# Reordering the score matmuls of a second attention stage, and splitting every other exponential in two

## The reference

```
qkv = xf @ W_qkv + b_qkv
q, k, v = split(qkv.reshape(B, N, 8, 96))
attn = softmax(einsum('bihd,bjhd->bijh', q, k) * 32 ** -0.5, axis=2)
res = einsum('bijh,bjhd->bihd', attn, v).reshape(B, N, 256) @ W_out + b_out + xf
```

## Time and profile before

| | us |
|---|---|
| median of 3 runs | 1339.67 |
| lowest and highest of the runs | 1337.60, 1340.34 |
| the profiled execution | 1338.09 |
| its span, first to last instruction | 1336.3 |
| TensorE, VectorE, ScalarE, GpSimd busy | 1258.8, 779.1, 813.4, 685.3 |

### The profile page before, as it was taken

The page is one execution under the profiler, slowest core; times in us unless marked ns, Lnnn a source line. Parts: engine busy times, 40 slices in busy tenths (PEclk is TensorE's granted clock), DMA queues, the critical chain, the costliest instruction groups (busy, mean ns, idle before and its releaser), DMA issues.

```text
span 1336.3 us, 24965 instructions
## 1 busy us (share of the span) xinstructions
PE 1258.8 (94%) x10420; PEld 495.7 (37%) x10420; DVE 779.1 (58%) x1002; ACT 813.4 (61%) x912; POOL 685.3 (51%) x387
## 2 busy tenths in 40 slices
PE   6499999999999999999999998879999899999987
PEld 4332222222222222222222224634444655555543
DVE  6766666666666666666666665620002677777753
ACT  4677777787777778777777874442212355555552
POOL 3466666666666666666666663320000066656562
PEclk9599999999999999999999999989999999999999
DMA  2340111011011101101100100000006222222211
GB/s 73 96 135 1 33 32 25 9 33 33 1 33 33 24 10 33 32 2 33 33 24 10 33 1 1 0 0 0 0 1 229 93 53 56 57 57 57 67 27 71
DMA packets 22504, 51.63 MB, mean 39 GB/s; under 512 B 5622, under 2 KB 10870, under 8 KB 22264
## 3 DMA queue, kind: packets, MB, share of 16 engines
q1 hardware_dynamic: 20084, 43.74, 11.8%
q10 hardware_dynamic: 2308, 6.30, 1.9%
HBM read 36.64 MB, written 11.15 MB: 36 GB/s over the span
## 4 chain that ended last, share of the span: by engine, by line
PE 86%; ACT 6%; DVE 5%; issue 1%; DMA 1%; ACTq 0%; POOL 0%; POOLq 0%; SPq 0%; DVEq 0%
PE ps L936 33%; PE ps L945 18%; PE ps L1131 6%; PE ps L927 5%; ACT big L619 5%; PE ps L1142 5%; PE ps L1043 4%; PE ps L1053 4%; PE ps L1152 2%; PE ps L1072 2%; PE ps L1082 1%; PE ps L1030 1%; PE ps L1195 1%; DVE big L669 1%; PE ps L996 1%
## 5 line engine op out<-in xcount | busy, mean ns | idle before, releaser
L936 PE MATMUL ps<-big,w 64*64 64x512 f32 x4096 | 483.5, 589 | 0.0
L534 ACT ACTIVATE big<-ps 128x1024 f32<-128x1024 f32 x256 | 261.9, 1023 | 178.5 <-PE ps L936 178.5
L728 DVE TENSOR_SCALAR big<-big 128x1024 f32<-128x1024 f32 x256 | 177.7, 694 | 263.9 <-POOL big L435 263.9
L435 POOL TENSOR_TENSOR big<-qpad 128x1024 f32<-128x1024 f32 x128 | 244.6, 1911 | 146.5 <-PE ps L936 70.4
L722 DVE TENSOR_TENSOR big<-qpad,ps 128x1024 f32<-128x1024 f32 x256 | 310.9, 1215 | 7.3 <-ACT ps L513 5.4
L435 POOL TENSOR_TENSOR big<-qpad,V 128x1024 f32<-128x1024 f32 x128 | 244.4, 1910 | 129.4 <-PE ps L936 72.3
L534 ACT ACTIVATE big<-ps,vec 128x1024 f32<-128x1024 f32 x256 | 283.7, 1108 | 0.0
L945 PE MATMUL ps<-big,w3s 128*32 128x512 f32 x2048 | 246.2, 598 | 1.3 <-ACT big L534 1.3
L936 PEld LDWEIGHTS ps<-big,w 64*64 64x64 f32 x4096 | 146.5, 133 | 206.5 <-issue 112.4
L460 POOL TENSOR_TENSOR big<-big 128x1024 f32<-128x1024 f32 x32 | 76.2, 2382 | 238.6 <-ACT big L619 189.4
L619 ACT ACTIVATE big<-ps 128x1024 f32<-128x1024 f32 x128 | 130.9, 1024 | 107.4 <-PE ps L1131 90.9
(11 more groups left out here) (154 smaller groups left out, 977.7 us busy)
## 6 DMA issues: line engine op xcount, KB each, us to landing
raw<-s_f SPq DMA_DIRECT2D x32, 512.0 KB, 5.9
h1l<-k_d SPq DMA_DIRECT2D x33, 128.0 KB, 3.5
h1h<-q_d ACTq DMA_DIRECT2D x33, 128.0 KB, 4.1
X<-in_x SPq DMA_DIRECT2D x2, 1024.0 KB, 6.2
q_d<-XN SPq DMA_DIRECT2D x4, 512.0 KB, 3.2
k_d<-XN SPq DMA_DIRECT2D x4, 512.0 KB, 3.7
q_d<-big SPq DMA_DIRECT2D x4, 512.0 KB, 3.9
k_d<-big SPq DMA_DIRECT2D x4, 512.0 KB, 5.0
```

The source lines that it names most:

```text
L435: pool.tensor_tensor(h1[m % HRING].rearrange("p (y a b) -> p y a b", y=2, b=W), u.unsqueeze(2).to_broadcast(shape), a[:, :, HALF // W * hf ...
L534: act.activation(h2[m % H2RING], z2[m % ZRING], ACT.Relu, bias=v("cb2") if m % 2 else 0.0).then_inc(h2_ready, 1)
L728: dve.tensor_scalar(h1[m % HRING], h1[m % HRING], 0.0, None, ALU.max).then_inc(h1_ready, 1)
L936: last = pe.matmul(z2[m % ZRING][CH * y:CH * (y + 1), HALF * x:HALF * (x + 1)], w2[CH * x:CH * (x + 1), :], h1[m % HRING][CH * x:CH * (x + ...
```

## The change

The order of a round becomes across(2r), along(2r+14), across(2r+1), along(2r+15). The three pairs of banks still rotate by one with every product, so that the pairs are dealt out anew: along(2r+15) now takes the pair of across(2r), across(2r+1) that of the round before's along(2r+13), and along(2r+14) that of the round before's across(2r-1). In the rounds without along the two across slots take different pairs. The exponential of every even slot becomes two, of 128 x 512 each; the first signals a new semaphore `half_ready`, the second `pr_ready`. The two matmuls of an odd along wait for one of them each. The waits of across, along and turn are rewritten for the new pairs.

```diff
@@ -196,7 +196,7 @@
         vv_ready, vv_saved = sem("vv_ready"), sem("vv_saved")
         rT_in = [sem(f"rT_in{i}") for i in range(2)]
         st_in = [sem(f"st_in{i}") for i in range(HEADS3)]
-        added, sums_done = sem("added"), sem("sums_done")
+        added, sums_done, half_ready = sem("added"), sem("sums_done"), sem("half_ready")
         tr_ready, m_hi, m_lo, m_in, ones_ready, bo_ready, bo_saved = (
             sem(x) for x in ("tr_ready", "m_hi", "m_lo", "m_in", "ones_ready", "bo_ready", "bo_saved"))
         sc_ready, mx_ready, st_ready, pr_ready, pv_done, o_done = (
@@ -236,7 +236,7 @@
             if x < AHEAD_MAX:
                 return (x + turned(x)) % 2
             s = x - AHEAD_MAX
-            return (4 * (s // 2) + s % 2 + turned(x - x % 2)) % 3
+            return (4 * (s // 2) + 2 * (s % 2) + turned(x)) % 3
 
         def turn_pair(n):
 
@@ -245,7 +245,7 @@
 
         def across_pair(s):
 
-            return (4 * (s // 2) + 3 * (s % 2) + turned(s - s % 2 + AHEAD_MAX) - 1) % 3
+            return (4 * (s // 2) + 2 * (s % 2) + turned(s + AHEAD_MAX) - 1) % 3
 
         def plane_rows(t, first, n, a):
 
@@ -616,7 +616,11 @@
                 if s >= PRING:
                     act.wait_ge(pv_done, s - PRING + 1)
                     act.wait_ge(added, (s - PRING) // 2 + 1)
-                act.activation(PT[s % PRING], bank(2 * across_pair(s), 2), ACT.Exp).then_inc(pr_ready, 1)
+                if s % 2 == 0:
+                    act.activation(PT[s % PRING][:, 0:HALF], bank(2 * across_pair(s)), ACT.Exp).then_inc(half_ready, 1)
+                    act.activation(PT[s % PRING][:, HALF:N], bank(2 * across_pair(s) + 1), ACT.Exp).then_inc(pr_ready, 1)
+                else:
+                    act.activation(PT[s % PRING], bank(2 * across_pair(s), 2), ACT.Exp).then_inc(pr_ready, 1)
                 if s % NK == NK - 1 and HEADS3 <= s // NK + 3 < G:
                     load_queries(s // NK + 3)
 
@@ -1095,14 +1099,14 @@
                 elif x < 2:
                     pass
                 elif turning(x):
+                    pe.wait_ge(mx_ready, x)
+                elif x == AHEAD_MAX:
+                    pe.wait_ge(mx_ready, x - 1)
+                elif x % 2 == 0:
                     pe.wait_ge(pr_ready, x - AHEAD_MAX)
-                elif turning(x - 1):
-                    pe.wait_ge(m_lo, turned(x))
-                elif x % 2 == 0:
-                    pe.wait_ge(mx_ready, x - (x == AHEAD_MAX))
-                elif x > AHEAD_MAX + 1:
-                    pe.wait_ge(pr_ready, x - AHEAD_MAX - 1)
                 for hf in range(2):
+                    if x > AHEAD_MAX and x % 2 == 1:
+                        pe.wait_ge((half_ready, pr_ready)[hf], ((x - AHEAD_MAX + 1) // 2, x - AHEAD_MAX)[hf])
                     last = pe.matmul(bank(2 * along_pair(x) + hf), QS[n % HEADS3][0:ROWS, P * it:P * (it + 1)],
                                      KS[n % HEADS3][0:ROWS, HALF * hf:HALF * (hf + 1)], start=True, stop=True)
                 last.then_inc(sc_ready, 1)
@@ -1110,7 +1114,10 @@
             def turn(n):
 
                 pe.wait_ge(mx_ready, NK * (n + 1))
-                pe.wait_ge(mx_ready, min(TURN + NK * n - 1, SLOTS))
+                if n < G - 1:
+                    pe.wait_ge(mx_ready, TURN + NK * n - 1)
+                else:
+                    pe.wait_ge(pr_ready, TURN + NK * n - AHEAD_MAX - 2)
                 pe.transpose(bank(2 * turn_pair(n))[0:NK, 0:P], amax[n % HEADS3][:, :], ident[:, :]).then_inc(tr_ready, 1)
 
             def across(s):
@@ -1119,14 +1126,16 @@
                 if kt == 0:
                     pe.wait_ge(m_in, 32 * (n + 1))
                 x = s + AHEAD_MAX
-                if s % 2 == 1:
+                if turning(x):
                     pe.wait_ge(pr_ready, s)
-                elif x <= SLOTS:
-                    pe.wait_ge(mx_ready, x if turning(x) or s == 0 else x - 1)
-                else:
+                elif turning(x - 1):
+                    pe.wait_ge(m_lo, turned(x))
+                elif s == 0:
+                    pe.wait_ge(mx_ready, AHEAD_MAX)
+                elif s > 1 and x - 1 <= SLOTS:
+                    pe.wait_ge(mx_ready, x - 1)
+                elif s > 1:
                     pe.wait_ge(pr_ready, s - 2)
-                    if x == TURN + NK * (G - 1) + 4:
-                        pe.wait_ge(m_lo, G)
                 for hf in range(2):
                     last = pe.matmul(bank(2 * across_pair(s) + hf), KS[n % HEADS3][0:ROWS + 2, P * kt:P * (kt + 1)],
                                      QS[n % HEADS3][0:ROWS + 2, HALF * hf:HALF * (hf + 1)], start=True, stop=True)
@@ -1166,16 +1175,14 @@
             pe.wait_ge(vv_saved, 2 * NK)
             pe.wait_ge(ones_ready, 1 + HEADS3)
             for r in range(SLOTS // 2 + 2):
-                s, x = 2 * r, 2 * r + AHEAD_MAX
-                if turning(x):
-                    turn(turned(x) - 1)
-                if s < SLOTS:
-                    across(s)
-                if x < SLOTS:
-                    along(x)
-                    along(x + 1)
-                if s < SLOTS:
-                    across(s + 1)
+                for s in (2 * r, 2 * r + 1):
+                    x = s + AHEAD_MAX
+                    if turning(x):
+                        turn(turned(x) - 1)
+                    if s < SLOTS:
+                        across(s)
+                    if x < SLOTS:
+                        along(x)
                 if 0 < r <= SLOTS // 2:
                     weigh(2 * r - 2)
                     weigh(2 * r - 1)
```

## The result

The changed kernel takes 1319.9 us (median of four runs, 1316.65 to 1320.53) against 1338.95 for the kernel before in the same comparison (median of four, 1337.6 to 1340.34). The ratio is 0.9853, 95% interval 0.9833 to 0.9872: 19.05 us faster. The forecast was 18.8 us and 1320.9. The profiled execution of the changed kernel took 1319.84 us, its span is 1317.2.

A forecast was written before the change was run, and what follows sets the result against it. Taken as the bound: the exponential of across(2r), for which across(2r+1) waits. Gains of 8.8 + 0.8 + 9.2 = 18.8 us against the median of 1339.67 gave 1320.9 us, range 1314 to 1328.

The forecast's parts named there:

- What bounds the kernel: Second attention: across(2r+1) waits for the exponential of across(2r), which sets the 3.94 us round; along products cost nothing.
- Order and banks in rounds 2 to 56: Rounds with along: by the new order alone nothing is won; the wait moves from across(2r+1) to along(2r+15).
- The two halves: Rounds 2 to 56: only the second along matmul waits, weigh starts at 2.34 not 2.50; 0.16 us a round, 8.8 us.
- The two terms on which it rests: Even exponentials: a half takes some 0.60 us, and halves start 0.49 us apart.
- Halves without overlap: Rival, even exponentials: each half pays its whole 0.60, 0.05 us won a round, 1326.9 us; chance 0.11.
- Halves as cheap as the whole: Rival, even exponentials: two halves cost as much as the whole, 0.23 us won a round, 1317.0 us; chance 0.09.
- the slower case: Rival, even exponentials: TensorE writing the neighbouring bank slows the halves, weigh 0.30 us later than today, 1346.2 us; chance 0.04.
- its estimate of 1.13 us for the two: Even exponentials by the skill's formula: halves take 1.13 us instead of 1.09, a round wins 0.12, kernel some 2 us later.
- Rounds 0 and 1: First rounds wait for VectorE, 0.49 and 0.32 us; new order wins 0.8 us, between 0 and 1.0.
- Rounds 57 on: Rounds without along: across(2r+1) starts without a wait, rounds of 2.57 us instead of 3.94; 9.2 us won to the last sums.
- GpSimd did not hold these rounds: Rival, rounds without along: GpSimd, 2.36 of 2.57 us, or an overlooked wait holds them at 3.94, 1330.1 us; chance 0.06.
- What moves with it: Other engines in the new order: VectorE's load 2.90 us a round against 3.78; key and query loads get more slack.

The follow-up runs named there:

- experiment 4: Changed kernel, with the first matmul of an even across signalling by itself so the first half exponential starts early: 1306.77 us, ratio to before 0.9761.
- experiment 2: Kernel before, in its order and banks, with even exponentials in halves and across(2r+1)'s two matmuls waiting for one half each: 1327.73 us, ratio 0.9924.
- experiment 3: Changed kernel, with both matmuls of the odd along waiting for the second half of the exponential: 1332.13 us, ratio to before 0.9955.
- experiment 1: Changed kernel's new order and banks, but every exponential whole and one wait for the odd along: 1329.98 us, ratio to before 0.9935.
- 5: Kernel before, in its order and banks, with halved even exponentials and the early signal from the first across matmul: 1319.47 us, ratio 0.9851.
- 7: Kernel before's order with halves and early signal, without query loads after the third head (those results left out): 1317.19 us, ratio to before 0.9843.

## Why the prediction was right

**What bounds the kernel**: right. The end of the exponential, not TensorE's load, set the round; experiment 4 takes 0.23 of the 0.26 us of wait away by moving that end alone, and experiment 2, with 3.77 us for rounds with and without along, shows that along was free in the old order.

**Order and banks in rounds 2 to 56, nothing won**: right, 3.94 us with the order alone. **The two halves, 0.16 a round**: right, 0.17, so 9.4 us for 8.8. The two terms on which it rests were read from other activations of the trace and held: halves of 0.598 and 0.592 us (mean) that start 0.49 to 0.50 apart, against 0.60 and 0.49. The lengths are means over the whole stage, with columns as in the earlier trace rows:

```profile
L620 ACT ACTIVATE big<-ps 128x512 f32<-128x512 f32 x64 | 38.3, 598 | 81.9 <-PE ps L1140 81.9
L621 ACT ACTIVATE big<-ps 128x512 f32<-128x512 f32 x64 | 37.9, 592 | 0.0
```

The same rows settle three rivals. Halves without overlap would have started 0.60 apart. Halves as cheap as the whole would have ended at 1.79. And the slower case, a conflict with TensorE's write into the neighbouring bank, would show in the second half, during which the first along matmul runs (from 1155.33): it is not longer than the first. The Trainium skill's 93 ns of overlap (ScalarE: Activation LUTs, the section on ACT_TABLE_LOAD's cost) agrees with the 0.10 seen here; its fixed part is a little too high for this shape: its estimate of 1.13 us for the two compares with 1.09 measured. The Trainium skill's rule of the Read-Write Bubble (Advanced Engine Details and Errata, The Read-Write Bubble), taken as no overlap between instructions, is not borne out at 128 x 512; what a split does cost is 0.07 us (experiment 3).

**Rounds 0 and 1, 0.8 us**: 1.0, at the upper bound. The two waits for VectorE, 0.49 and 0.32, went whole, not in part: with the order alone experiment 1 wins 0.83 there. The other 0.2 is the halves, which shorten round 1 as well (from 3.54 in experiment 1 to 3.36), and the prediction had not counted them there. **Rounds 57 on, 9.2 us**: 9.15, with 2.56 to 2.58 us for a plain round, and 0.47 in rounds 57 and 58 for the turn where I had put 0.45. GpSimd did not hold these rounds, but with 0.18 us of idle time it is the next that would.

**What moves with it**: the prediction called the earlier key and query loads more slack, with no wait in sight, and put no price on it. Experiments 4, 5 and 7 show that this slack, and the new banks, become worth some 5 us as soon as rounds shrink to 3.5 us. VectorE's 2.90 us a round was an average: a round with two reciprocals holds 1.16 + 1.23 + 0.54 + 0.55 = 3.48 us of its work (timeline of the fifth kernel), which leaves room at 3.77 and next to none at 3.5.

## What to carry to other kernels

Take out one engine's work in the mind, or find a stretch where some of it is absent: if the period stays, as in the earlier trace rows, that work is not on the path, however busy its engine looks. Where two engines hand a tile back and forth, signal each half in both directions: the consumer's first half can start with the producer's first matmul, and only the last piece stays on the path. Rotating buffers should be dealt out so that no product takes those of its direct predecessor on the slow path; but work moved into a wait must not change the kind of matmul, or the price of that change has to be set against the wait.

## What was not expected

Another pair of changes between the 128-column score matmuls and the 32-column fp32 matmuls cost 0.31 us of TensorE (1.00 - 0.89 and 0.67 - 0.47), more than the 0.26 us wait that it was to fill. The two kinds differ in columns and in type, and no run tells which of the two costs it. And with rounds at 3.5 us two waits came up at once in the old order, loads and VectorE, where the waits of along in the late rounds named the loads alone: taking these away gave back 2.3 us, not the 5.4 that were put down to them.
